# A gated cross-attention and mixture-of-experts layer on one core: expert blocks of 128 rows with stationary activations, expert weights split once, a gather at the end in place of accumulating stores, the shared expert last

## The reference

```
x = x + tanh(g_xattn) * xattn(layernorm(x), ctx, pos, pos, Wq, Wkv, Wout, bout)   # 32 heads of 16, axial rope
h = layernorm(x)
shared = (silu(h @ s1g.T) * (h @ s1u.T)) @ s2.T                  # inner width 704
probs = softmax(h @ gate_w.T)                                    # 16 experts, the best 6 kept, not renormalised
moe = sum over the kept experts e of probs[e] * ((silu(h @ w1g[e].T) * (h @ w1u[e].T)) @ w2[e].T)   # width 352
out = x + tanh(g_ffn) * (moe + shared)
```

## Time and profile before

| | us |
|---|---|
| median of 3 runs | 1760.6 |
| lowest and highest run | 1755.97, 1762.88 |
| profiled execution: span from first to last instruction | 1759.8 |
| from the start to the end of phase A (all engines meet) | 755.4 |
| phase B, 64 blocks | 1004.4 |
| TensorE busy | 1599.8 (91%) |
| VectorE, ScalarE, GpSimd busy | 979.1 (56%), 774.8 (44%), 795.2 (45%) |
| DMA | 265.9 MB, mean 151 GB/s |

### The profile page before, as it was taken

How to read it: one execution, slowest core, us unless ns; L and a number is a source line. 1 busy time by engine, 2 the same in 40 slices (tenths; PEclk the granted TensorE clock), 3 DMA queues, 4 the chain that set the end, 5 groups by cost and what they waited for, 6 DMA issues and landing times.

```text
span 1759.8 us, 33331 instructions
## 1 busy us (share of the span) xinstructions
PE 1599.8 (91%) x10754; PEld 1364.4 (78%) x10754; DVE 979.1 (56%) x1828; ACT 774.8 (44%) x1262; POOL 795.2 (45%) x817
## 2 busy tenths in 40 slices
PE   4999999999999999758899899988899998899897
PEld 3677777777777776558888888888888888888886
DVE  4766666666566654345555455555555555555453
ACT  4444444444444443144444444444444444444442
POOL 3423333333333321315555555555555555555554
PEclk8899999999999998879999999999999999999999
DMA  6001111221111111498777777778777777777774
GB/s 227 10 7 59 59 62 67 74 72 71 60 58 58 49 50 50 152 324 248 213 213 213 205 209 211 211 219 219 209 205 209 207 203 217 218 216 217 198 201 71
DMA packets 93980, 265.90 MB, mean 151 GB/s; under 512 B 9905, under 2 KB 11954, under 8 KB 85106
## 3 DMA queue, kind: packets, MB, share of 16 engines
q1 hardware_dynamic: 67826, 205.75, 36.2%
q0 software_dynamic: 26112, 59.62, 16.4%
HBM read 191.78 MB, written 73.55 MB: 151 GB/s over the span
## 4 chain that ended last, share of the span: by engine, by line
DMA 25%; issue 8%; PE 8%; DVE 8%; ACT 4%; POOL 2%; DVEq 1%; SPq 0%; POOLq 0%; ACTq 0%
DMA out<-y,row_id 22%; PE bank L1330 5%; DVE y L1399 3%; DVE act_f L1388 3%; DMA xr<-expert_rows 2%; ACT silu L1258 2%; PE bank L1344 2%; POOL out L1295 2%; ACT act_hi L1261 2%; PE bank L1316 1%; DMA expert_rows<-pad_row 0%; DVE row_w L1383 0%; DVE row_id L1384 0%; ACTq L99 0%; DVEq L99 0%
## 5 line engine op out<-in xcount | busy, mean ns | idle before, releaser
L1295 POOL DMA_INDIRECT out<-y,row_id x128 | 310.5, 2426 | 417.8 <-DVE y L1399 394.1
L1330 PE MATMUL bank<-xe_hi,w_hi 128*128 128x256 f32 (+1 forms) x1536 | 441.2, 287 | 0.0
L1330 PE MATMUL bank<-xe_lo,w_hi 128*128 128x256 f32 (+1 forms) x1536 | 434.4, 283 | 0.0
L1330 PE MATMUL bank<-xe_hi,w_lo 128*128 128x256 f32 (+1 forms) x1536 | 433.6, 282 | 0.0
L1261 ACT ACTIVATE act_hi<-act_f 128x256 fp32r<-128x256 f32 (+1 forms) x192 | 80.1, 417 | 473.0 <-DVE act_f L1388 473.0
L1330 PEld LDWEIGHTS bank<-xe_hi,w_hi 128*128 128x128 f32 (+1 forms) x1536 | 286.1, 186 | 0.0
L1330 PEld LDWEIGHTS bank<-xe_lo,w_hi 128*128 128x128 f32 (+1 forms) x1536 | 285.0, 186 | 0.0
L1330 PEld LDWEIGHTS bank<-xe_hi,w_lo 128*128 128x128 f32 (+1 forms) x1536 | 284.5, 185 | 0.0
L1368 DVE TENSOR_TENSOR w_lo<-w_raw,w_hi 128x2816 fp32r<-128x2816 f32 x64 | 197.9, 3092 | 55.6 <-ACT w_hi L1244 55.6
L1279 POOL TENSOR_TENSOR w_lo<-w_raw,w_hi 128x1024 fp32r<-128x1024 f32 x64 | 190.1, 2970 | 34.1 <-ACT w_hi L1254 34.1
L1316 PE MATMUL bank<-const,xr 128*128 128x128 f32 x512 | 80.9, 309 | 107.5 <-DMA xr<-expert_rows 105.2
(11 more groups left out here) (189 smaller groups left out, 3229.2 us busy)
## 6 DMA issues: line engine op xcount, KB each, us to landing
w_raw<-in_w SPq DMA_DIRECT2D x66, 1408.0 KB, 8.1
xr<-expert_rows SPq DMA_DIRECT2D x64, 530.0 KB, 3.6
w_raw<-in_w SPq DMA_DIRECT2D x66, 512.0 KB, 4.4
w_raw<-in_w SPq DMA_DIRECT2D x66, 192.0 KB, 5.0
expert_rows<-pad_row SPq DMA_DIRECT2D x13, 530.0 KB, 6.1
x_sb<-in_x SPq DMA_DIRECT2D x16, 256.0 KB, 3.6
x_res<-in_x SPq DMA_DIRECT2D x16, 256.0 KB, 4.3
out<-x SPq DMA_DIRECT2D x16, 256.0 KB, 2.0
```

Of the source, the lines that this page charges most:

```text
L1295: g_.indirect_dma_start(out_rows, bass.IndirectOffsetOnAxis(row_id[j][:, s, :].bitcast(U32), 0), y[j][:, s, :], None, compute_op=ALU.add). ...
L1330: last = nc.tensor.matmul(bank[2 + c][0:m, half * BLOCK:(half + 1) * BLOCK], w[j][:, d, col:col + m], xx[j][:, d, :], start=(k == 0), stop ...
```

## The change

BLOCK becomes 128, so there are 112 blocks. In a block the activations are stationary and the weights move, 352 columns at a time: gate and up halves go to two banks, 24 matmuls. The hidden values are scaled by the routing weight, transposed on PE (3 transposes), split, and multiplied in 9 matmuls of 512 columns. Weights are loaded and split once for each of the 18 experts (16 and the two halves of the shared one) into two slots; POOL issues the loads and does both halves of the split. The columns of a block's slot come from the table by register. ACT copies the result out of PSUM and SP stores it in `y_rows`, 128 rows in a row; no DMA accumulates. After the routed blocks the shared expert runs as 32 steps (two for each batch), while POOL gathers each token's six rows (96 indirect DMAs) and DVE adds them up with the row saved by phase A. Phase A loses the shared expert; it stores x1 and the normalised rows. The first two experts' weights are split by POOL in phase A.

The core of the diff (semaphore declarations, buffers, constants, table arithmetic and the shared expert's deleted code are left out):

```diff
-BLOCK = 256
-SUB = BLOCK // P
+BLOCK = 128
+SLOTS = 2
+TILES = BLOCKS + BATCHES
+STEPS = BLOCKS + SHARED * BATCHES
...
+        def split_w(pool, e):
+            s = e % SLOTS
+            pool.wait_ge(w1_in, 16 * (e + 1))
+            pool.wait_ge(w2_in, 32 * (e + 1))
+            for c, (_, m) in enumerate(WC):
+                nc.gpsimd.tensor_copy(w2_hi[c][0:m, s * D:(s + 1) * D], w2_raw[0:m, c, :]).then_inc(w_hi_made, 1)
+            for d in range(DC):
+                for half in range(2):
+                    nc.gpsimd.tensor_copy(w1_hi[d][half][:, s * WIDTH:(s + 1) * WIDTH],
+                                          w1_raw[:, d, half * WIDTH:(half + 1) * WIDTH]).then_inc(w_hi_made, 1)
+            pool.wait_ge(w_hi_made, 11 * (e + 1))
...
@@ phase A, POOL
                     scatter(*at(PLACE))
-                if at(PROJECT) and isinstance(at(PROJECT)[0], int) and at(PROJECT)[0] < SHARED:
-                    split_shared(at(PROJECT)[0])
+                    if isinstance(at(PLACE)[0], int) and at(PLACE)[0] == BATCHES - 3:
+                        split_w(pool, 0)
+                        pool.wait_ge(w_made, 8)
+                        load_w(nc.gpsimd, 1)
+                    if isinstance(at(PLACE)[0], int) and at(PLACE)[0] == BATCHES - 1:
+                        split_w(pool, 1)
...
@@ phase B, POOL
-                for s in range(SUB):
-                    waits_apart(pool, passed, (y_done, SUB * g + s + 1))
-                    g_.indirect_dma_start(out_rows,
-                                          bass.IndirectOffsetOnAxis(row_id[j][:, s, :].bitcast(U32), 0),
-                                          y[j][:, s, :], None, compute_op=ALU.add).then_inc(added[j], 16)
+            for e in range(2, EXPERTS + SHARED):
+                pool.wait_ge(w_made, 8 * e)
+                if e == 4:
+                    find_rows_of_y()
+                load_w(nc.gpsimd, e)
+                last = BLOCKS if e == EXPERTS + SHARED - 1 else \
+                    pool.value_load(ends_i[0:1, e - 2:e - 1], min_val=1, max_val=BLOCKS)
+                waits_apart(pool, passed_pool, (y_mm, last))
+                split_w(pool, e)
...
+            for b in range(BATCHES):
+                need(pool, comb_done, b - 1)
+                for k in range(TOPK):
+                    nc.gpsimd.indirect_dma_start(gath[b % 2][:, k, :], None, y_rows,
+                                                 bass.IndirectOffsetOnAxis(y_slots[:, b * 8 + k:b * 8 + k + 1], 0))\
+                        .then_inc(gathered[b % 2], 16)
...
@@ phase B, PE
+                pe.wait_ge(x_lo_done, t + 1)
+                need(pe, act_done, g)
+                pe.wait_ge(w_made, ready)
+                for d in range(DC):
+                    for xx, w in ((x_hi, w1_hi), (x_hi, w1_lo), (x_lo, w1_hi)):
+                        for half, to in enumerate((g_bank, u_bank)):
+                            last = nc.tensor.matmul(to[:, 0:WIDTH], xx[jt][:, d, :], w[d][half][:, cols],
...
+            def one_step(i, at):
+                if i == 0:
+                    transpose_x(0, 0, 0)
+                if live(i, -2):
+                    down(i, at)
+                if starts_tile(i, 1):
+                    transpose_x(*tile(i, at, 1))
+                if live(i, -1):
+                    transpose_act(*at(-1))
+                if live(i, 0):
+                    up(i, at)
...
@@ phase B, SP, before the first step
+            for t in range(2):
+                load(t, t, 0)
...
+            pads(range(4, EXPERTS))
...
+                if i == 0:
+                    load(2, 0, 1)
+                    sp.wait_ge(pads_out[0], 16 * 6)
+                    for k in range(1, EXPERTS // 4):
+                        sp.wait_ge(pads_out[k], 16 * 4)
```

More of the change, by code:

```diff
@@ L200, in phase_a @@
+def phase_a(nc, sb, sem, bank, const, ident, table, table_dram, table_p, table_in, ends_i, pad_at, pads_out,
+            slots_all, y_step, tanh2, scattered, load_w, split_w, w_made, twice,
+            x, ctx_t, pos, wq, wkv, wout, bout, gates, gate_w, cf, rows, x1_rows, x2_rows):
     with ExitStack() as st:
@@ L1165, in phase_b @@
[L1165 to L1176 removed]
+        xr = two("xr", [P, ROW])
@@ new lines, in store, with load_x1 @@
+            def store(t, j, n):
+                waits_apart(sp, passed, (y_done, t + 1))
+                sp.dma_start(y_blocks[t], y[j][:]).then_inc(y_out[j], 16)
+            def load_x1(b):
+                need(sp, comb_done, b - 1)
+                sp.dma_start(x1_t[b % 2][:], x1_rows[b]).then_inc(x1_in[b % 2], 16)
+            sp.wait_ge(table_in, 16)
+            for k in range(2):
+                sp.wait_ge(scattered[k], 16 * TOPK * BATCHES // 2)
+            sp.wait_ge(pads_out[0], 16 * 4)
@@ new lines, in _ @@
+            for t in range(2):
+                load(t, t, 0)
+            sp.wait_ge(pad_zero, 1)
+            for e in range(2):
+                sp.dma_start(rows[EXPERTS * CAP + e * BLOCK:EXPERTS * CAP + (e + 1) * BLOCK, :], pad_row[:])\
+                    .then_inc(pads_out[0], 16)
+            pads(range(4, EXPERTS))
[5 more added lines that the diff above has]
+                        sp.wait_ge(pads_out[k], 16 * 4)
+                if live(i, -2) and routed(i, -2):
+                    store(*at(-2))
+                if i is None or starts_tile(i, 1):
+                    t, j, n = tile(i, at, 1)
+                    if not isinstance(t, int):
+                        load(*at(3))
+                    elif t + 2 < TILES:
+                        load(t + 2, j, n + 1)
+                if i is not None and i >= BLOCKS - 2 and (i - BLOCKS) % 2 == 0 and (i - BLOCKS) // 2 + 1 < BATCHES:
+                    load_x1((i - BLOCKS) // 2 + 1)
+                if i is not None and i - 3 >= BLOCKS and ends_tile(i, -2):
+                    b = tile_of(i - 2) - BLOCKS
+                    sp.wait_ge(y_done, BLOCKS + b + 1)
+                    sp.dma_start(out[b], o_t[b % 2][:]).then_inc(o_out[b % 2], 16)
@@ L1349, in one_round, with transpose_x @@
-            def one_round(at):
-                for stage, work in ((PREPARE, prepare), (INNER, inner), (OUTER, outer)):
-                    if at(stage):
-                        work(*at(stage))
-            rounds(pe, BLOCKS, DEPTH, PEELED, one_round)
+            def transpose_x(t, j, n):
+                pe.wait_ge(x_in[j], 16 * (n + 1))
+                need(pe, x_lo_done, t)
+                for c in range(DC):
+                    last = nc.tensor.transpose(x_bank[:, c * P:(c + 1) * P], xr[j][:, c * P:(c + 1) * P], ident)
+                last.then_inc(x_mm, 1)
@@ new lines, in transpose_act, with down @@
+            def transpose_act(g, j, n):
+                pe.wait_ge(act_done, g + 1)
+                need(pe, a_lo_done, g)
+                for c in range(3):
+                    last = nc.tensor.transpose(a_bank[:, c * P:(c + 1) * P], act[j][:, c * P:(c + 1) * P], ident)
+                last.then_inc(a_mm, 1)
+            def down(i, at):
+                g, j, n = at(-2)
+                t, jt, nt = tile(i, at, -2)
+                if routed(i, -2):
+                    off = pe.value_load(table[0:1, bass.ds(g * T_N + T_W2, 1)], min_val=0, max_val=D)
+                    cols = bass.ds(off, D)
+                    first = final = True
+                else:
+                    s = (i - 2 - BLOCKS) % SHARED
+                    cols = slice(s * D, (s + 1) * D)
+                    first, final = s == 0, s == SHARED - 1
+                pe.wait_ge(a_lo_done, g + 1)
+                if first:
+                    need(pe, y_done, t)
+                for c, (_, m) in enumerate(WC):
+                    for k, (l, w) in enumerate(((a_hi, w2_hi), (a_hi, w2_lo), (a_lo, w2_hi))):
+                        last = nc.tensor.matmul(y_bank[:], l[j][0:m, c, :], w[c][0:m, cols],
+                                                start=(first and c == 0 and k == 0),
+                                                stop=(final and c == 2 and k == 2))
+                last.then_inc(y_mm, 1)
@@ L1410 @@
+            steps(dve, one_step)
 def kernel(**inputs):
@@ L1443 @@
         "w2": w2p.reshape(-1, 3, P, D),
[L1444 to L1445 removed]
+        "cf": constants(),
     }
```

748 lines of the change are left out of this document (321 added, 427 removed).

## The result

The changed kernel takes 1808.9 us (median of 4 runs, 1808.7 to 1811.1) against 1758.3 before (1754.2 to 1762.9): ratio 1.0264 [1.0215, 1.0313], slower by 2.6% (the quotient of these two medians is 1.029; the experiments are compared by the first number). The forecast was 1737 in a range of 1665 to 1805; the result lies above the range and on the other side.

The account below looks back on a forecast made before the run. TensorE was taken to bound phase A and the accumulating output adds to pace phase B. Phase A 663 us plus phase B 1074 (30 + 110 x 7.2 + 21 + 223 + 8) gave 1737, range 1665 to 1805.

Parts of the forecast that it names:

- The round of phase A: Steady round of phase A without the shared expert: 35.6 us instead of 42.2, saving 92 us over 14 rounds.
- the middle: Phase A round: 35.6 us, between 32 at full clock and 40; clock falls in about half the rounds or stretch.
- R3: Rival, slower: the clock falls in every round of phase A, 40 us a round, 61 us more, 1798; chance 0.11.
- The end of phase A: From scatter 13's last issue to the engines' meeting: 64 us as before, as 23 + 21 + 20; phase A 663 us.
- the split of expert 1: End of phase A, on POOL: 20 us, taking the place of its last wait of 18.73 us.
- Splits: An expert's weights split on POOL, half subtractions and half casts: 20 us (15 to 27), casts taken as 8 us.
- The block step: Routed block of phase B: 4.04 + 2.29 + 0.87 = 7.2 us for 128 rows, 112 blocks, 806 us.
- R2: Rival, slower: register work on TensorE's queue in phase B costs 1.33 us a block, 149 us, 1886; chance 0.14.
- The loads: Three table loads a block on TensorE's queue: 0.93 us if its sequencer can't run ahead.
- the operations among the matmuls: 15 register operations a block on TensorE's queue: between nothing and 2.5 us, taken as 0.4.
- The standstill: TensorE stands still about 21 us for expert 17's weights, whose slot the last routed block frees.
- the shared steps: Shared expert at the end of phase B: 32 steps, 13.9 us for each two, 223 us.

Follow-up runs that it names:

- e2_fill2: e1_fill plus 6 more needless matmuls of 512 columns ahead of the row's transposes at u = 5; ratio 1.0128 to the kernel before the change.
- e1_fill: The changed kernel plus 8 needless matmuls of 512 columns at u = 5 of each phase A round; ratio 1.0108 to the kernel before the change.
- e9_giveback: The changed kernel plus needless matmuls at u = 5, 6 and 7 in the shared expert's number and widths, 12.4 us a round; ratio 1.0442 to the kernel before.
- e4_split1: The changed kernel with expert 1's split as POOL's first work of phase B instead of its last of phase A; ratio 1.0173 to the kernel before.
- e5_static: The changed kernel with one fixed tile as TensorE's moving operand in routed blocks, so no table loads or register operations there; ratio 0.9936 to the kernel before.
- e11_hoist: The changed kernel with the two table loads for `up` read at the start of the step, ahead of `down`; ratio 1.0070 to the kernel before.

## Why the prediction was wrong, step by step

**The round of phase A: the step that failed.** The forecast took "the middle" between 32 us (clock full) and 40 (clock falls in every round). The clock fell in every round, and the rounds are 41.0, a little over R3, which had 0.11. In the terms of the sum, a round was 29.0 us of work, 3.0 of idle time and 3.6 for the clock; of the 41.07 us measured, 2.5 are idle and 38.6 busy, so the first two were right and the clock took 9.6 us (R3 had it at 8). From the first batch's row transposes to the last one's it is 606.1 us before and 580.9 after: 25 us saved where 92 were forecast, which makes 67 of the 80 us missed in phase A. The start (6 us) and what comes after the last row transposes (145.6 us in place of 138.9, 7 us) make up the rest.

The idle time was of the forecast size, but not where I had put it: 1.94 us hang on ScalarE's copy of q_t, which I had not looked at, and the row comes 0.95 us late in every second round, not 1.7 in each. What I had wrong was the part of the gaps: I priced whether gaps of that length bring the clock down, and e2_fill2 shows it down without a gap of that kind, once the wide matmuls of u = 6 and 7 are away. Which property of the narrow matmuls does it isn't shown; the runs show where it falls (the gate's matmuls in e1_fill and e2_fill2, and where any fall is left in e9_giveback) and that wide ones in their number and places bring it back. Rows that I had read spoke for it: in the earlier trace rows TensorE was busy 10.06 of 10.20 us at 0.50, and half of each round became such a stretch. The right forecast from them was R3.

**The end of phase A.** I had 64 us from the last scatter of batch 13 to the meeting, before and after. It was 64.0 before and 74.1 after (668.9 to 742.9). From scatter 13 to the root chain it took 27.2 us (POOL stood 8.9 of them behind the split of expert 0 and the loads), where I had 23; chain and scatters took 22.0 (21), the split of expert 1 16.0 (20). The term that was left out is the last: I let the split of expert 1 take the place of POOL's wait of 18.73 us, and missed that some 9 us pass on POOL after its last instruction before the phase can end. Before, its last issue ended at 736.6 and SP held the end, at 755.1, so they were covered. e4_split1 shows the split's 16 us exposed in full. Splits themselves were cheaper than forecast (16.0, not 20), as the one-input half of the rule in the Trainium skill (GPSIMD Engine Reference, 4.1 Engine selection) would have had it: a cast took 1.20 ns a column, near the 1.10 of DVE's subtraction.

**The start.** The first row transposes come at 16.4 us instead of 10.4, 6 us that I had not looked for. In the other runs of kernels derived from the change they come at 13.8 to 15.7. The cause wasn't tried and stays open.

**The block step: right by two errors.** 7.2 was forecast and 7.24 measured, but not by my terms. The matmuls and transposes take 6.70 (e5_static): 0.5 less than my sum, which had 4.04, 2.29 and 0.87 where the trace has 3.93, 2.09 and 0.68. All three were read in groups of the kernel before with what lay around them, for `down` I took more than half of 4.37, and twice 2.01 is 4.02, not 4.04. R2's mechanism, which I had put at 1.33 us, is there with 0.54, and filled the hole. It was not a rival to be set against the forecast but a term that belonged in it: 60 us. The loads, put at 0.93, cost about 0.50; the operations among the matmuls, put at 0.4, cost 0.03. What spoke against it, that transposes and `down` give the sequencer 3 us of work ahead, covers a part: the loads stand behind a wait that the sequencer meets first, so in the block named under e11_hoist they start only 1.4 us ahead of the last transpose, and with range operations and waits they need 1.85. That the forecast of the block came out is luck.

**The standstill and the shared steps.** 15.4 against 21 and 13.3 against 13.9: the mechanisms were right, the sizes 5 us and 10 us too high, from the over-priced split and block terms. Nothing waited at the 16 expert changes beyond 1.8 us in 7 waits.

**Where the gain of the blocks went.** By the measured parts, the routed half of phase B fell from 1004 to about 835 us (1064 less 16 x 13.3 and the 15.4): 169 us gained, where 174 were forecast (1004 less 1074 - 223 - 21). The shared expert at the end costs 213 + 15 us, and phase A became 13 shorter (755.4 - 742.9), start and end with all that changed there included. By these numbers that exchange is the whole loss: 228 - 13 - 169 = 46 of the 47 us. A kernel with the new blocks and the shared expert left in phase A wasn't tried.

## What to carry to other kernels

Work that keeps TensorE wide between narrow stages may cost nearly nothing where it stands and its full price where it is moved to; before counting what its removal saves, look in the trace for a stretch of the same stage without it, and take the clock of that stretch as the forecast. On a sequencer, count what stands behind the last wait ahead of a matmul, not how many instructions there are: two 0.3 us loads moved ahead of the wait were worth 34 us here, while 15 register operations among the matmuls had cost 0.03 us a block. Where a wait is listed from the modelled end of a matmul, take the distance of the starts, with and without what you suspect. When a sum comes out right, check its terms one by one, since two errors of 0.5 us had cancelled here.

## What the runs showed of the hardware that I had not expected

TensorE's granted clock was 0.50 in a stretch in which it was busy all 8.00 of 8.00 us (e2_fill2, 482 to 490), with transposes of 128 columns and attention of 32 rows in it, behind the gate's matmuls of 16 columns. In e2_fill2 the fall began at these matmuls in nearly every round, with no gap over 0.24 us in the microseconds ahead of them; needless matmuls of 512 and 352 columns brought the mean back to 0.98 (e9_giveback).

POOL needed 8.7 to 9.0 us from the end of its last instruction or DMA issue to the start of the next phase wherever it was the last to arrive: 9.01 in the changed kernel and in all eight variants that keep the split there, 8.67 without it (e4_split1).

And a pair of table loads of 0.30 us each on TensorE's queue, behind a wait, delayed a block by more than the waits listed for it: 25.3 us were listed as waits on the issue, 58 went when the register work was taken out.
